# The head of a Mamba-like mixer makes the experts' rows of two batches instead of one, with a new table of places

## The reference

```python
x = x + 0.5 * ffn(layernorm(x), gate_w, experts)
x = x + mixer(layernorm(x), W_in, conv_w, conv_b, A_log, D, W_out)
x = x + 0.5 * ffn(layernorm(x), gate_w, experts)
```

```python
x_conv = silu(causal_conv4(ssm) + conv_b)
delta  = softplus(x_conv)
A_d    = exp(delta[..., None] * -exp(A_log))        # 16 states a channel
h      = A_d * h + x_conv**2 ; y = x_conv * sum(h)  # a scan over 2048 tokens
out    = (y * silu(res) + D * x_conv) @ W_out.T
```

## Time and profile before

| | |
|---|---|
| median of 3 runs | 3703.75 us (3695.53 to 3709.73) |
| profiled execution | 3714.21 us, its span 3712.6 us |
| VectorE busy | 3117.0 us (84%) |
| TensorE busy | 2790.2 us (75%) |
| ScalarE busy | 2127.8 us (57%) |
| GpSimd busy | 1321.5 us (36%) |
| the 512 scans (L1182) | 2224.3 us busy, first at 448.0, last at 2930.9 |
| DMA engines, software queue | 51.9% of their time |

### The profile page before, as it was taken

One profiled execution on the slowest core, in us unless ns is written; L12 is line 12 of the kernel. 1 busy time (PEld: TensorE's weight loads), 2 busy tenths in 40 slices (PEclk: granted clock), 3 DMA queues, 4 the chain that ended last, 5 costly groups with the idle time before them and its releaser, 6 DMA issues. The chain is left out here.

```text
span 3712.6 us, 29747 instructions
## 1 busy us (share of the span) xinstructions
PE 2790.2 (75%) x9252; PEld 1532.0 (41%) x9252; DVE 3117.0 (84%) x2640; ACT 2127.8 (57%) x2285; POOL 1321.5 (36%) x894
## 2 busy tenths in 40 slices
PE   8702688889889889988978978998897796035553
PEld 4501343345346345434534634543452455024442
DVE  6797479999999999999999999999999667982222
ACT  5300467876877877688687787778767362001111
POOL 0002265346245344534624534460111100036665
PEclk9655799999899899999989989998998896567776
DMA  6202278688778878867877787885676571034666
GB/s 265 117 0 80 68 174 182 142 174 181 156 167 165 178 163 179 193 134 170 182 161 170 160 178 162 175 193 119 126 150 132 113 283 81 0 117 145 206 220 241
DMA packets 146178, 575.61 MB, mean 155 GB/s; under 512 B 22096, under 2 KB 73872, under 8 KB 99216
## 3 DMA queue, kind: packets, MB, share of 16 engines
q0 software_dynamic: 76704, 400.61, 51.9%
q1 hardware_dynamic: 69360, 173.68, 12.6%
HBM read 154.72 MB, written 119.60 MB: 74 GB/s over the span
## 5 line engine op out<-in xcount | busy, mean ns | idle before, releaser
L1182 DVE TENSOR_TENSOR_SCAN state<-state,drive 128x2048 f32<-128x2048 f32 x512 | 2224.3, 4404 | 51.5 <-ACT state L1388 51.0
L1388 ACT ACTIVATE state<-delta,neg_a 128x2048 f32<-128x2048 f32 x512 | 1019.5, 2005 | 208.0 <-DMA delta<-xc 83.3
L1639 PE MATMUL ps_states<-state,ident 128*128 128x512 f32 x1792 | 847.5, 618 | 81.2 <-DMA state<-state 64.0
L1067 POOL DMA_DIRECT2D state<-state x255 | 235.7, 926 | 1306.1 <-DVE state L1182 1286.8
L1541 PE MATMUL ps_proj<-x1t,w_in 128*128 128x512 f32 x1024 | 515.9, 650 | 92.2 <-ACT res L1337 33.7
L1639 PEld LDWEIGHTS ps_states<-state,ident 128*128 128x128 f32 x1792 | 345.1, 198 | 481.4 <-issue 381.0
L1557 PE MATMUL ps_proj<-conv_in,tap 128*128 128x512 f32 x1024 | 487.8, 627 | 56.6 <-ACT conv_in L1301 35.3
L996 POOL DMA_INDIRECT picked<-normed_rows,slot_now x112 | 355.1, 3170 | 100.9 <-PE ps_rows L1522 56.0
L1541 PEld LDWEIGHTS ps_proj<-x1t,w_in 128*128 128x128 f32 x1024 | 207.2, 207 | 379.0 <-issue 276.7
L1012 POOL DMA_INDIRECT x<-routed_rows,row_now x112 | 344.2, 3074 | 34.8 <-issue 34.8
L1557 PEld LDWEIGHTS ps_proj<-conv_in,tap 128*128 128x128 f32 x1024 | 204.0, 202 | 321.7 <-issue 280.5
(11 more groups left out here) (298 smaller groups left out, 3253.1 us busy)
## 6 DMA issues: line engine op xcount, KB each, us to landing
state<-state POOLq DMA_DIRECT2D x255, 1024.0 KB, 7.1
delta<-xc POOLq DMA_DIRECT2D x24, 1024.0 KB
normed_rows<-rows_in SPq DMA_DIRECT2D x8, 2048.0 KB
x_rows<-x SPq DMA_DIRECT2D x16, 1024.0 KB, 7.7
normed_rows<-rows_mid SPq DMA_DIRECT2D x8, 2048.0 KB
f_total<-x_rows SPq DMA_DIRECT2D x8, 2048.0 KB
routed_rows<-f_routed SPq DMA_DIRECT2D x128, 128.0 KB
out<-f_total SPq DMA_DIRECT2D x8, 2048.0 KB
```

Source lines behind the costliest of these rows:

```text
L1067: nc.gpsimd.dma_start(out=state[held(q)][:], in_=state[held(q - 1)][:], accum_op=ALU.add).then_inc(pair_landed(b, q // 2)[0], 16)
L1182: nc.vector.tensor_tensor_scan(state[held(q)][:], state[held(q)][:], drive[j % 2][:], 0.0, ALU.mult, ALU.add).then_inc(state_ready, 1)
L1388: nc.scalar.activation(state[held(q)][:], delta[j % 2][:], ACT.Exp, scale=g.neg_a[:, j, n:n + 1]).then_inc(decay_ready, 1)
L1639: mm = nc.tensor.matmul(ps_sum[c][:], g.ident[:], state[held(q)][:, c * CH:(c + 1) * CH], start=(opening and n == 1), stop=(n == N - 1))
```

## The change

**Two batches in the head.** The head's loops over slots run over 2 x 16 slots instead of 16. Slots 16 to 31 are batch 1's: their picked rows go to `delta0` and `delta1`, their results to `xc2` and `xc3`, their stores to a second table `routed_rows1` with a semaphore of its own, which `bring_back` of batch 1 reads. All that made batch 1's slots inside batch 0 goes: the picks, `fill_first`, SP's stores and expert loads, `set_slots(1)`. Counts of semaphores shift by one batch. The code of bodies 1 to 7 is the same but for the tables.

**New places.** WHEN, the table of the chunks' slots, and eleven others change in part; two rows of WHEN are shown.

```diff
-    FFN, FIRST_FFN = 41, 0
+    FFN = 41
-    STATS = (27, 36)
-    COPY_OUT, ADD_OUT = (9, 11, 12, 16, 17, 19, 22, 24), (7, 11, 13, 15, 15, 19, 23, 25)
+    STATS = (27, 35)
+    COPY_OUT, ADD_OUT = (9, 11, 13, 17, 17, 19, 22, 24), (7, 9, 13, 15, 17, 19, 25, 27)
-    BEGIN = (7, 8, 8, 8)
-    GATE, COMBINE = (3, 3, 4, 4), (6, 4, 6, 4)
+    BEGIN = (7, 6, 8, 7)
+    GATE, COMBINE = (3, 3, 4, 4), (7, 6, 6, 4)
-    STEP = {9: 1, 27: 2, 43: 3, 59: 4}
+    STEP = {9: 1, 25: 2, 43: 3, 59: 4}
-    SCALE = (29, 38)
-    TURN = {31: (0, 1), 33: (2, 3), 37: (4, 5), 39: (6, 7)}
-    TURNED = {36: (0, 1), 41: (2, 3), 43: (4, 5), 45: (6, 7)}
+    SCALE = (30, 37)
+    TURN = {29: (0, 1), 33: (2, 3), 35: (4, 5), 39: (6, 7)}
+    TURNED = {36: (0, 1), 40: (2, 3), 43: (4, 5), 45: (6, 7)}
...
-    PICKED, ROUTED, BROUGHT, NORMED = 0, 2, 4, 0
+    PICKED = (state[0], state[1], delta[0], delta[1])
+    ROUTED = (state[2], state[3], xc[2], xc[3])
+    BROUGHT, NORMED = (state[4], state[5]), (state[0], state[1])
...
-        ("ssm", 3): (27, 33, 33, 34),
+        ("ssm", 3): (27, 32, 34, 35),
-        ("res", 3): (32, 32, 34, 35),
+        ("res", 3): (33, 33, 35, 36),
...
     def at_slot(v, start, end, first, more, last):
-        if first and 0 <= v - FIRST_FFN < end:
-            return 1, v - FIRST_FFN
...
         def body(b, first, more, last):                  # SP
-            if first:
-                sp.wait_ge(x1_joined, T)
-                sp.sem_inc(g.passed_sp, 1)
-                load_expert(b + 1, 0)
-                load_expert(b + 1, 1)
             for s in range(SL):
-                if not last and (first or s >= EARLY):
+                if not (first or last) and s >= EARLY:
                     store_slots(b + 1, s)
...
-        for s in range(SL):                              # SP, head
-            e, h = s // NH, s % NH
+        for s in range(2 * SL):
+            e, h = s % SL // NH, s % NH
             sp.wait_ge(routed_scaled, s + 1)
-            sp.dma_start(routed_v[e, ...], early(ROUTED, s)).then_inc(routed_out[s % NY], 16)
+            if s < SL:
+                sp.dma_start(routed_v[e, ...], early(ROUTED, s)).then_inc(routed_out[s % NY], 16)
+            else:
+                sp.dma_start(next_routed_v[e, ...], early(ROUTED, s)).then_inc(next_routed_out, 16)
...
             if t == 0:                                   # GpSimd, bring_back
                 pool.wait_ge(rows_set, nb)
-                for i in range(NY):
-                    pool.wait_ge(routed_out[i], (nb + 1) * 16 * (SL // NY))
+                if isinstance(nb, int) and nb == 1:
+                    pool.wait_ge(next_routed_out, SL * 16)
+                else:
+                    for i in range(NY):
+                        pool.wait_ge(routed_out[i], nb * 16 * (SL // NY))
...
         def body(b, first, more, last):                  # GpSimd
-            if first:
-                for s in range(NX + 4 - FIRST_FFN):
-                    pick(b + 1, s)
...
-                for v in (q, q + 1):
-                    if first and NX <= v < SL + FIRST_FFN - 4:
-                        pick(b + 1, v + 4 - FIRST_FFN)
...
-        for s in range(SL):                              # GpSimd, head
+        for s in range(2 * SL):
             nc.gpsimd.indirect_dma_start(
                 out=early(PICKED, s), out_offset=None, in_=g.normed,
-                in_offset=bass.IndirectOffsetOnAxis(ap=g.slot_token[:, 0, s:s + 1].bitcast(U32), axis=0)
+                in_offset=bass.IndirectOffsetOnAxis(ap=g.slot_token[:, s // SL, s % SL:s % SL + 1].bitcast(U32), axis=0)
             ).then_inc(early_pick_in[s // 2], 16)
...
-        for s in range(SL + 1):                          # ScalarE, and TensorE alike, head
-            if s < SL:
+        for s in range(2 * SL + 1):
+            if s < 2 * SL:
                 act.wait_ge(pick_turned, s + 1)
...
-                    if first:                            # TensorE, body
-                        fill_first(q + NS - 1)
```

62 lines of the change are left out of this document (28 added, 34 removed).

## The result

The changed kernel took 3721.91 us (median of 5 runs, 3717.61 to 3729.63) against 3703.75: a ratio of 1.0058, 95% interval 1.0040 to 1.0076. It is slower, where the forecast was faster, 3668 us with a range of 3655 to 3684; the measured time also lies outside the 3643 to 3693 that was to hold eight times in ten.

What follows compares the result with a forecast made beforehand. VectorE was taken as the bound, with only its idle time and the first scan's start open to change. Head +2.8, first batch -17.5 and tables -21.0 gave -35.7: 3703.75 to 3668 us, range 3655 to 3684.

Steps and rivals of the forecast that it cites:

- Part 1: First batch: picks leave GpSimd's queue, state additions are issued earlier, VectorE's idle time falls from 26.2 to 8.7 us; -17.5.
- Rival C: First batch: the 13.16 us wait is TensorE's and ScalarE's chain and largely stays, gain only 5; 3680 us, chance 0.10.
- Part 2: Head: 16 more gathers and slots ahead of the first scan delay bringing back from 381.6 to 384.4; +2.8 us.
- the 456: Head: a first scan beyond 456 us would show the forecast wrong; it was expected between 448 and 454.
- the cover worked out to 0.7 us: Head: the 16 extra slots on TensorE and ScalarE are just hidden before ScalarE's next work at 398.3, 0.7 us to spare.
- the prediction's case without late gathers: Head: without the 2.8 us gather delay, the extra slots would be the bound, at +2.1 us.
- The estimate of one gather in 2.27 us: Head: gathers beside back-to-back L658 on VectorE have a pitch of 2.27 us instead of 1.25; five lose 1.0 each.
- the row of 1.50 us: Head: profile row at 357.96, a gather taking 1.50 us instead of 0.95 beside L658, read as evidence against the skill's rule.
- Part 3: Tables in every batch: new places remove VectorE waits, 3.5 us in each of batches 2 to 7; -21.0 us.
- the step now goes ahead of it: Middle batches: unit 2's step moves from 27 to 25, ahead of a state addition; ScalarE's wait ends some 1.2 us earlier.
- the hold (5.2 us): Middle batches: the step waits for soft_done in GpSimd's queue, making gathers, state addition and x addition up to 5.2 us later.
- rival D: Middle batches: GpSimd's 5.2 us at the step delays the state addition and decay 32; slower, 3725 us, chance 0.06.

Runs made afterwards that it cites:

- e6_late: Kernel before with batch 1's 16 gathers issued in the head behind the bringing back, their slots' work staying in the first batch; 0.9989 of before.
- e4_plain: Changed kernel with batch 1's 16 gathers in the head replaced by plain DMAs of SyncE's queue from consecutive rows; 1.0002 of before.
- r_after: The changed kernel again, unedited, in a calm set (one without the stall); 1.0006 of before.
- r_before: The kernel before, profiled again in a calm set; head 104.4 us, first batch 326.4, batches 2 to 7 311.2 on average.
- e7_again: Second run, in a calm set, of the changed kernel with the second step's addition put back to position 27; 0.9961 of before.
- e12_rest: Kernel before, head and first batch as they were, with all new tables except STEP, which stays at 27; stalling set, 0.9997 of before.
- e7_step: Changed kernel with one table entry put back, the second step's addition at position 27 instead of 25; calm set, 0.9958 of before.

## Why the prediction was wrong

- **Part 1, the first batch (-17.5): right in size, partly by luck.** Measured -17.9, and -16.9 in a calm set. The first addition is issued 9.35 us behind the first scan (487.06 - 477.71), as put. The reason was less than half right: e6_late gives the gathers 4 to 7 of it and TensorE's and ScalarE's slot work, which the sum left out, the other 10 to 13. Rival C's chain was real; the change just removed it too.
- **Part 2, the head (+2.8): the term that was mis-sized, and where most of the loss is.** It measured +34.2 in the first comparison and +10.1 calm, and put the first scan at 477.7, far beyond the 456 that was named as a sign of being wrong. The failed step is the time at which rows are ready: the sum took 381.60 for it, the start of the bringing back, 47.3 us behind the rank table. That was a number of the stalling condition, whose mark is in the trace of before as well: VectorE's 3.09 and 1.61 <-remote of the earlier trace rows and this wait of ScalarE, which I read without asking what they were:
```profile
360.28 0.37 ACT L1440 COPY picked_t<-ps_states 128x256 f32<-128x256 f32 x1 [5.28 <-remote]
```
Calm, the rows are ready at 41.1 and the 32 gathers end at 49.2, so the bringing back moves by 8.5 us where the sum had 2.8. The second failed step is the cover worked out to 0.7 us (396.2 of slots under 397.6): with the stall, ScalarE was still at its slots and came to the deviation 98.9 us behind the rank table (428.54), where the sum had 64.0 (398.3). Calm, at 63.7, the cover held; and e4_plain is the prediction's case without late gathers, where the slots are the bound at +2.1: it measured +2.3.
- **The gathers beside L658.** The estimate of one gather in 2.27 us came out. In r_after, while L658 runs back to back:
```profile
352.25 1.96 POOL L1089 DMA_INDIRECT state<-normed_rows,slot_token  x1 [0.30 <-issue]
354.51 1.96 POOL L1089 DMA_INDIRECT state<-normed_rows,slot_token  x1 [0.30 <-issue]
356.78 1.97 POOL L1089 DMA_INDIRECT state<-normed_rows,slot_token  x1 [0.30 <-issue]
```
The first 16 gathers take 1.54 us on average there, the other 16, behind L658, 0.95; but r_before's 16 take 1.43, so the change pays only 1.7 us of this. It is not the stall, in which L658 itself hardly runs. The Trainium skill (SBUF — State Buffer, section Who interferes with whom), quoted in Part 2, puts the contention on GpSimd's reads and infers that writing descriptors for a DMA isn't held. The prediction took the row of 1.50 us as being against it, but a gather also reads its 128 places, from `slot_token` in SBUF, which the prediction left out. In the kernel after, 178 issues of indirect DMAs began while a scan, an op with two SBUF inputs, had at least 1.5 us to run: all ended 0.79 to 0.89 us behind that scan's end. Of 273 issues of DMAs without such places (DMA_DIRECT2D) under the same condition, all ended before it, after 0.85 to 1.61 us. So the trace agrees with the rule and with the inference; that it is the reading of the places that waits, no run shows by itself.
- **Part 3, the tables (-21.0): wrong in sign, measured +9.3, and +7.7 calm.** The failed step is "the step now goes ahead of it", the order with the state addition. Ahead of it the step gained 0.9 us on average, and GpSimd stood 5.8 to 7.2 us, because the logarithm ends 130.7 to 133.2 us into the batch and GpSimd is there at 126.5. The prediction had the hold (5.2 us), but took only 1.7 us off a batch's gain for it and put it on gathers and statistics. It left out the state addition two positions on, issued 7.7 us later, on which TensorE's projections and then the deviation hang. Of rival D the hold and the late addition came true, its last link did not: decay 32 starts 151.7 us into the batch before and 151.4 after. D's 3725 is near the measured 3721.9 partly by luck: its middle batches were priced at 5.2 us each and cost 1.6, its head at +8 and cost 34.2.
- With STEP at 27 much of Part 3's reading holds: the waits by scans 34 and 35 are gone, the deviation's is 0.4 us a batch (e7_again), and decay 34 starts 157 to 160 us into the batch, where the prediction had 158 to 159. What it had at nothing is new waits, 2.0 us ahead of scan 26 and more at scans 41 to 43 (2.7 us on average, where 43 and 44 had 1.8).
- Two slips of arithmetic change nothing: five gathers that lose 1.0 us each end at 384.8, not 384.4, and the 0.74 for faster holds all of rival C, not most of it.
- COMBINE took L1163's wait away, as put, and one of 1.0 us for another operand came after scan 19. Without STEP the tables are worth 1.6 us a batch (e12_rest), not 3.5.

In the stalling condition e7_step's parts would be about +34 - 18 - 4, 12 us slower than before: an estimate from the table, not run. So STEP explains the middle batches, and the head's stall, whose cause is open, adds 24 of the 34 us that the head lost in the first comparison.

## What to carry to other kernels

A DMA issue that waits for another engine is placed in a queue by when its input is ready, not by when its output is wanted: too early, it comes no sooner and holds all that stands behind. Before a cover of under a microsecond is believed, every gap near it that the profile puts to "remote" or "issue" has to be explained, in the trace of before. And where a change adds up from several edits, undo them one at a time: here one number of the tables turned no gain into one of 0.4% in calm runs, though alone it costs the kernel before only 0.14%. It did not decide the first comparison, where the head's stall weighed more.
